# One value product instead of three for the chunk of four left-over keys in a three-layer decoder kernel

## What is computed

```python
xn = _layernorm(x, gamma_media, beta_media)          # context, 6404 rows
ln = _layernorm(latents, gamma_lat, beta_lat)        # the 1024 tokens
q = ln @ Wq + bq
kv_input = jnp.concatenate([xn, ln], axis=1)
kv = kv_input @ Wkv + bkv
k, v = jnp.split(kv, 2, axis=-1)
sim = jnp.einsum('bhid,bhjd->bhij', q * DH ** (-0.5), k)
attn = jax.nn.softmax(sim, axis=-1)
out = jnp.einsum('bhij,bhjd->bhid', attn, v)
```

## Time and profile before

| | us |
|---|---|
| median of 3 runs | 1928.13 |
| lowest and highest run | 1924.66, 1931.77 |
| profiled execution, first to last instruction (span) | 1921.9 |
| TensorE busy in the span | 1815.2 (94%) |
| VectorE busy | 1529.5 (80%) |
| ScalarE busy | 1111.2 (58%) |

### The profile page before, as it was taken

The page is one execution under the profiler, slowest core; times in us unless marked ns, Lnnn a source line. Parts: engine busy times, 40 slices in busy tenths (PEclk is TensorE's granted clock), DMA queues, the critical chain, the costliest instruction groups (busy, mean ns, idle before and its releaser), DMA issues.

```text
span 1921.9 us, 32146 instructions
## 1 busy us (share of the span) xinstructions
PE 1815.2 (94%) x9267; PEld 908.2 (47%) x9267; DVE 1529.5 (80%) x2457; ACT 1111.2 (58%) x1368; POOL 252.0 (13%) x321
## 2 busy tenths in 40 slices
PE   4888889999999999999999999999999999996997
PEld 3775334444444444444444444444444444443554
DVE  6875788888888888888878787879797979546776
ACT  3233256666666666666666666666666666674554
POOL 3911397000000000000000000000000000001554
PEclk7987799999999999999999999999999999997999
DMA  4001020000000000000000000000000000000000
GB/s 124 1 11 33 17 66 21 1 0 0 0 0 0 0 0 0 0 0 0 0 0 0 0 0 0 0 0 0 0 0 0 0 1 0 1 0 1 1 0 11
DMA packets 15350, 13.89 MB, mean 7 GB/s; under 512 B 5839, under 2 KB 13779, under 8 KB 14934
## 3 DMA queue, kind: packets, MB, share of 16 engines
q1 hardware_dynamic: 15318, 13.48, 2.3%
HBM read 12.96 MB, written 0.52 MB: 7 GB/s over the span
## 4 chain that ended last, share of the span: by engine, by line
PE 86%; DVE 8%; issue 3%; ACT 2%; DVEq 0%; DMA 0%; POOLq 0%; POOL 0%; ACTq 0%
PE PS L1105 86%; ACT p_arena L614 1%; DVE mxs L914 1%; DVE w_arena L789 1%; ACT p_arena L607 1%; DVE w_arena L805 0%; DVE mxs L988 0%; DVE w_arena L798 0%; DVE z_arena L1055 0%; DVE w_arena L819 0%; DVE st L867 0%; DVE st L721 0%; DVE w_arena L816 0%; DMA w_arena<-in_x 0%; DVE rs L700 0%
## 5 line engine op out<-in xcount | busy, mean ns | idle before, releaser
L604 ACT ACTIVATE p_arena<-PS 128x1024 f16<-128x1024 f32 (+1 forms) x480 | 484.4, 1009 | 544.3 <-PE PS L1105 544.1
L1105 PE MATMUL PS<-a_arena,z_arena 128*128 (+1 forms) x2832 | 746.4, 380 | 3.8 <-DVE a_arena L933 3.5
L1105 PE MATMUL PS<-p_arena,z_arena 128*128 128x512 f16 x2832 | 747.3, 379 | 1.4 <-ACT p_arena L614 0.3
L940 DVE TENSOR_TENSOR p_arena<-p_arena 128x1024 f16<-128x1024 f32 (+1 forms) x480 | 582.2, 1213 | 134.7 <-ACT p_arena L607 124.6
L914 DVE TENSOR_REDUCE mxs<-PS 128x512 f32 (+1 forms) x900 | 583.2, 667 | 101.1 <-PE PS L1105 98.8
L607 ACT ACTIVATE p_arena<-PS 128x1024 f32<-128x1024 f32 (+1 forms) x480 | 482.0, 1004 | 0.0
L1105 PEld LDWEIGHTS PS<-a_arena,z_arena 128*128 (+1 forms) x2832 | 275.0, 98 | 332.7 <-DVE a_arena L933 4.0
L1105 PEld LDWEIGHTS PS<-p_arena,z_arena 128*128 (+1 forms) x2832 | 272.3, 98 | 316.1 <-ACT p_arena L614 8.8
L1105 PE MATMUL PS<-z_arena,a_arena 128*128 (+3 forms) x1024 | 355.5, 364 | 15.4 <-DVE mxs L914 8.3
L478 POOL TENSOR_TENSOR z_arena<-z_arena 128x512 f16<-128x512 f32 x66 | 76.5, 1159 | 1505.5 <-ACT z_arena L663 1501.5
L1105 PEld LDWEIGHTS PS<-z_arena,a_arena 128*128 (+1 forms) x1024 | 99.0, 98 | 156.4 <-DVE mxs L914 25.1
(11 more groups left out here) (226 smaller groups left out, 965.2 us busy)
## 6 DMA issues: line engine op xcount, KB each, us to landing
w_arena<-in_L_ffn_gate_up_w SPq DMA_DIRECT2D x8, 512.0 KB, 3.7
p_arena<-in_ctx SPq DMA_DIRECT2D x2, 1600.0 KB, 8.4
w_arena<-in_L_ffn_down_w SPq DMA_DIRECT2D x8, 256.0 KB, 4.0
a_arena<-in_L_xattn_Wkv SPq DMA_DIRECT2D x1, 1024.0 KB, 6.7
w_arena<-in_x SPq DMA_DIRECT2D x1, 512.0 KB, 4.3
a_arena<-in_L_xattn_Wo SPq DMA_DIRECT2D x1, 512.0 KB, 7.2
p_arena<-in_L_xattn_Wq SPq DMA_DIRECT2D x1, 512.0 KB
out<-z_arena SPq DMA_DIRECT2D x8, 64.0 KB, 1.6
```

The source lines that it names most:

```text
L604: s.activation(Phi[:, r % 3, 0:w], ps, ACT.Exp, scale=1 / SSC).then_inc(hi_ready, 1)
L940: v.tensor_tensor(Plo[:, r % 3, 0:w], P32[:, r % 2, 0:w], Phi[:, r % 3, 0:w], ALU.subtract).then_inc(lo_ready, 1)
L1105: return t.matmul(o, l, r, start=start, stop=stop)
```

## The change

Chunk 0 holds its four keys three times: in rows 0 to 3, 32 to 35 and 64 to 67. In `Zhi` these rows hold the high part, the low part and the high part again; SyncE copies the two new strips inside the on-chip memory. In `ZThi` and `ZTlo` the four columns are written at columns 0, 32 and 64, so the scores and exponentials of the four keys come out three times too. VectorE then overwrites the third strip of `Phi` (rows 64 to 67) with the low part. One product of `Zhi` chunk 0 with `Phi` gives the three terms at once. It is issued in `values_low`; `values_high` leaves chunk 0 out. `Plo` of chunk 0 is not written any more, so the subtraction of step 0 covers 512 columns instead of 1024. Two semaphores are new: `left_st` (the strips have landed) and `left_lo` (the third strip of `Phi` is written, once per block).

```diff
-        zt_lo_v = sem("zt_lo_v")
+        zt_lo_v, left_st, left_lo = sem("zt_lo_v"), sem("left_st"), sem("left_lo")
...
+        def left_columns(zt):
+
+            return zt[:, 0:96].rearrange("p (g n) -> p g n", n=32)[:, :, 0:LEFT]
...
+            sp.wait_ge(z_lo, 1)
+            sp.dma_start(Zhi[32:32 + LEFT, 0, :], Zlo[0:LEFT, 0, :]).then_inc(left_st, 16)
+            sp.dma_start(Zhi[64:64 + LEFT, 0, :], Zhi[0:LEFT, 0, :]).then_inc(left_st, 16)
             sp.wait_ge(zlT_v, 2)
...
-                    s.copy(dst[:, c0 * P:c0 * P + n], PS[:, 2 + 2 * (i % 2) + o, 0:n]).then_inc(done, 1)
+                    ps = PS[:, 2 + 2 * (i % 2) + o, 0:n]
+                    if c0:
+                        s.copy(dst[:, c0 * P:c0 * P + n], ps).then_inc(done, 1)
+                    else:
+                        s.copy(left_columns(dst), ps.unsqueeze(1).to_broadcast([P, 3, LEFT])).then_inc(done, 1)
...
-                    cols = w * P if c0 else LEFT
-                    v.tensor_copy(ZTlo[:, c0 * P:c0 * P + cols], PS[:, 3 + 2 * (i % 2), 0:cols]).then_inc(zt_lo_v, 1)
+                    ps = PS[:, 3 + 2 * (i % 2), 0:w * P if c0 else LEFT]
+                    if c0:
+                        v.tensor_copy(ZTlo[:, c0 * P:(c0 + w) * P], ps).then_inc(zt_lo_v, 1)
+                    else:
+                        v.tensor_copy(left_columns(ZTlo), ps.unsqueeze(1).to_broadcast([P, 3, LEFT])).then_inc(zt_lo_v, 1)
...
                 dve.wait_ge(p32_ready, g + 1)
-                v.tensor_tensor(Plo[:, r % 3, 0:w], P32[:, r % 2, 0:w], Phi[:, r % 3, 0:w],
+                at = 0
+                if r == 0:
+                    at = QB
+                    rows = slice(64, 64 + LEFT)
+                    v.tensor_tensor(Phi[rows, 0, 0:QB], P32[rows, 0, 0:QB], Phi[rows, 0, 0:QB],
+                                    ALU.subtract).then_inc(left_lo, 1)
+                v.tensor_tensor(Plo[:, r % 3, at:w], P32[:, r % 2, at:w], Phi[:, r % 3, at:w],
                                 ALU.subtract).then_inc(lo_ready, 1)
...
                     o, first, _, zh, zl = sums(r, turn, i)
+                    if STEPS[r][i] == 0:
+                        continue
                     p = Phi[:, r % 3, i * QB:(i + 1) * QB]
...
-            def values_low(g, r, turn=0):
+            def values_low(g, r, turn=0, left=0):
 
                 pe.wait_ge(lo_ready, g + 1)
                 for i in range(len(STEPS[r])):
                     o, _, end, zh, _ = sums(r, turn, i)
+                    if STEPS[r][i] == 0:
+                        pe.wait_ge(left_lo, left + 1)
+                        mm(o, zh, Phi[:, 0, 0:QB], start=True, stop=False)
+                        continue
                     last = mm(o, zh, Plo[:, r % 3, i * QB:(i + 1) * QB], start=False, stop=end)
...
-                        values_low(lagged, lag)
+                        values_low(lagged, lag, left=j)
...
             pe.wait_ge(z_lo, N_HI + 1)
+            pe.wait_ge(left_st, 32)
             pe.wait_ge(a_lo, 2)
```

## The result

| | before | after |
|---|---|---|
| median of 22 runs, us | 1925.66 | 1921.63 |
| lowest and highest run | 1917.17, 1931.99 | 1909.28, 1927.02 |
| profiled span | 1921.9 | 1914.6 |

The ratio is 0.9973 with a 95% interval of 0.9960 to 0.9986. By the ratio that is 5.2 us less, with an interval of 2.7 to 7.7 us; the two medians lie 4.03 us apart. The interval leaves out 1, so the kernel is faster, but by less than the 0.5% that the prediction took as its bound, and by that bound it counts as no change, as forecast. The forecast was 6.1 us less and 1922.0 us.

A forecast was written before the change was run, and what follows sets the result against it. The prediction took TensorE's nearly gapless row of products as the bound, VectorE close behind. 6.9 - 0.3 - 0.5 = 6.1 us gain, from 1928.1 to 1922.0 us; range 1917 to 1930 us.

The forecast's parts named there:

- The price of a product: 512-column value products on TensorE cost 0.216 us each; two fewer save 0.43 us per block, 6.9 us in all.
- The place and the propagation: Products removed in step 2 start step 3 0.43 us sooner; the gain survives the next stop, nothing charged.
- The stop for the sums: TensorE's wait in step 2 for ScalarE's copy of the last block's sums, claimed to stay 0.23 us.
- the stop in the first turn: TensorE's wait for a maximum in the inner loop's first turn, claimed to stay 0.6 us.
- the first rival: Gain given back at the maxima, where VectorE doesn't arrive sooner: 1928.1 us, chance 0.13.
- The subtraction in two: Step 0's subtraction split on VectorE: 0.15 to 0.3 us more per block, hidden in fifteen blocks.
- The cover at the unit: Time between step 1's first maximum on VectorE and the TensorE unit needing it, put at 0.94 us.
- Block 0: First block, without cover at the maximum behind the subtraction: surplus of 0.3 us on the path, once.
- The new wait: Register wait on TensorE's sequencer: 0.03 us per block, 0.5 us in all, bounds 0 and 0.3 us per block.
- The second rival: Sequencer shows: the extra wait stops TensorE for 0.3 us per block, leaving 1.8 us gain, 1926.3 us; chance 0.08.
- Ahead of the blocks: SyncE's two extra transfers, some 0.3 us each, lie within its 80.8 us wait for POOL; costed at nothing.
- The third and fourth rivals: VectorE sets the pace: 1930.5 to 1932.9 us, chance 0.05; remaining product takes the others' time: 1928.1 us, chance 0.02.

The follow-up runs named there:

- v2: Changed kernel with units of the written-out steps 1,2,2,2,2,2,1 instead of 0,2,2,2,2,2,2, wait for A one step earlier: period 94.05 us, time 1924.08 us.
- v3: Changed kernel with units 2,2,2,2,2,2,0, so step 6 has none, and wait for A one step earlier: period 93.98 us, time 1922.17 us.
- v6: v1 with both units of step 6 behind both score groups: period 93.49 us, time 1912.86 us; timed ratio to the kernel before 0.9939.
- v7: v6 with v5's unit numbers, so three units in step 6: period 93.70 us, time 1916.32 us.
- three products again: Changed kernel with chunk 0's product issued three times, the two removed products back: period 94.28 us, time 1928.34 us.
- v1: Changed kernel with the second unit of step 2 ahead of the wait for the copied sums: period 93.71 us, time 1915.36 us.
- v5: v1 with units of the written-out steps 0,2,2,2,2,1,3, one more in step 6: period 93.70 us, time 1920.56 us.

## Why the prediction was right

**The price of a product.** Forecast 0.216 us, 0.43 us a block. The 15 periods give 6.46 / 15 = 0.431 us, and putting the products back gives 94.28 - 93.84 = 0.44 us. The 131 ns for a sustained stream that the Trainium skill gives ("TensorE: Matmul & The Clock Gate", "Back-to-back issue gap") are not borne out here: by them the estimate is 0.26 us a block.

**The place and the propagation.** The stop for the sums stayed 0.24 us and the stop in the first turn 0.60 us, so the first rival (given back at the maxima) is out. The chain of 3.85 us starts at TensorE's own scores. v2, v3 and v6 put numbers to it: with one product less behind those scores (v2) the stop is 0.22 us longer, with one more (v6) 0.21 us shorter. In v3 a unit less stands between the two score groups of step 6 as well, and the stop is v2's, so what counts is the work behind the scores. The prediction made the margin narrower than it was. It saw 0.04 us at 914.69, but VectorE waits for TensorE once more ahead of the stop, in step 5, before the change (first line) and after it (second line):

```profile
920.09 0.69 DVE L914 TENSOR_REDUCE mxs<-PS 128x1 f32<-128x512 f32 x1 [0.88 <-PE PS L1105]
915.88 0.69 DVE L928 TENSOR_REDUCE mxs<-PS 128x1 f32<-128x512 f32 x1 [0.89 <-PE PS L1125]
```

By these rows, a few hundredths lost at the first place would have been caught up at the second.

**The subtraction in two.** Forecast 0.15 to 0.3 us more on VectorE, hidden; measured 0.18 us, hidden in blocks 1 to 15. The overlap of neighbours, 0.07 us, is lost between instructions that begin at different partitions: 0.70 to 0.72 us from start to start, against 0.61 us between two strips at partition 64, and 0.61 us from the 128-row subtraction to the maxima behind it (903.83 to 904.44). With the rule that I cited from the Trainium skill ("VectorE: DVE Perf Modes", "Two Vector instructions with no wait between them") these traces agree. The cover at the unit was sized at 0.94 us ahead of the change, which left 0.94 - 0.18 = 0.76 us; the runs showed 0.67 us, so that term was a tenth of a microsecond too large.

**Block 0.** I charged 0.3 us, because no cover stands there. The changed kernel's profiled run shows none of it. From its timeline of block 0:

```profile
248.42 0.75 DVE L958 TENSOR_TENSOR p_arena<-p_arena 4x512 f16<-4x512 f32 x1 [4.80 <-ACT p_arena L618]
...
249.20 0.77 DVE L960 TENSOR_TENSOR p_arena<-p_arena 128x512 f16<-128x512 f32 x1
249.90 0.75 DVE L928 TENSOR_REDUCE mxs<-PS 128x1 f32<-128x260 f32 x2
250.37 0.29 PE L1125 MATMUL PS<-z_arena,a_arena 128*128 128x256 f16 x2 [1.11 <-DVE mxs L928]
```

The two instructions take 249.90 - 248.42 = 1.48 us, and the stop is 1.11 us where the earlier trace rows have 1.12. Before, the single instruction began at 248.70 and the maxima at 250.18, 1.48 us too. But other traces show the charge. Eight traces are of kernels with the same code up to this stop. In four of them (the changed kernel, v6 twice, v7) it is 1.10 to 1.13 us; in the other four (three products again, the run without the wait, v1, v5) it is 1.38 to 1.40 us, some 0.27 us more than before the change. From the run without the wait:

```profile
249.53 1.04 DVE L958 TENSOR_TENSOR p_arena<-p_arena 4x512 f16<-4x512 f32 x1 [4.80 <-ACT p_arena L618]
250.60 0.77 DVE L960 TENSOR_TENSOR p_arena<-p_arena 128x512 f16<-128x512 f32 x1
```

So the term is nothing in one half of the traces and of its forecast size in the other. What differs is what POOL, at work on the expert weights, is doing: where the strip takes 0.75 to 0.77 us it begins 0.2 us into a short instruction of POOL (line 476), where it takes 1.03 to 1.04 us 0.2 us into a longer one (line 480), and POOL's next instruction takes about twice its usual time in both. In the middle blocks, where POOL does nothing, a strip takes 0.68 us. That POOL is the cause was not tested. Block 0 gained 0.93 us in this trace, but its length was 98.91 us here and 99.80 us without the wait, so half a microsecond there means nothing.

**The new wait.** Charged 0.03 us a block, within 0 to 0.3; measured 0 by the run without it, within the 0.01 us that a period repeats to. The second rival is out.

**Ahead of the blocks.** SyncE's part of the timeline and its wait behind it:

```profile
103.11 0.69 SPq L364 DMA_DIRECT2D z_arena<-z_arena  x1
103.84 0.62 SPq L365 DMA_DIRECT2D z_arena<-z_arena  x1
185.24 0.35 SPq L373 DMA_DIRECT2D w_arena<-in_L_ffn_gate_up_w  x1
...
SPq L367 <- POOL z_arena L464: 80.2, 1, 80.2
```

Each issue took 0.65 us instead of the 0.3 us I wrote, and the wait behind them shrank from 80.8 to 80.2 us: hidden, as forecast.

**The third and fourth rivals** fall with the period of 93.84 us and with the two runs that put products in and take them out. **The numbers:** 6.1 us forecast; taken at their measured values the terms of the sum are 16 x 0.431 = 6.9 us, and losses of nothing or of 0.27 us in block 0. The ratio says 5.2 us with the forecast inside its interval, and the first and second rival (nothing and 1.8 us) outside. That the median came to 1921.63 us, within 0.4 us of the forecast 1922.0, is luck: the forecast started from a median of three runs, 1928.13 us, which is 2.5 us above that of 22, and the medians differ by 2.1 us less than the 6.1 us forecast. One reading of the text was off: I put 6.2 us around the span. The profiled run of the changed kernel took 1916.43 us with a span of 1914.6, so 1.8 us lie around it, and the rest was one run's distance from the median.

## What to carry to other kernels

When one engine issues without gaps, price an instruction by the distance between starts and check each later stop by asking where its chain begins: if it begins at that engine's own work, the stop moves along and the gain survives. Small operands can share a product across partition strips; the extra instruction elsewhere is free only up to the margin of the next consumer, which a run with the cost doubled or tripled measures directly. Stops are shortened by order rather than by amount: produce for the slow chain first and put independent work behind it.

## What the runs showed of the hardware that was not expected

The runs of one kernel differ by up to 18 us, and the blocks have next to no part in it: the 15 periods of v6 sum to 1382.30 us in both of its profiled runs. These two runs, of one kernel on two chips, have spans of 1911.0 and 1918.7 us, and the difference arises ahead of the blocks: the first score product of block 0 started at 243.74 us in the one and at 251.55 us in the other. Busy time by stretch from 100 to 180 us, first the shorter run, then the longer (length, TensorE, its weight loads, VectorE, ScalarE, POOL, granted clock, DMA):

```profile
100.00:180.00 80.00, 70.16 (x356) 52.48 (x355) 52.94 (x177) 23.52 (x75) 11.67 (x12) 0.79 0.02 7
```

```profile
100.00:180.00 80.00, 68.44 (x307) 49.35 (x306) 50.84 (x166) 19.27 (x63) 10.69 (x11) 0.74 0.02 7
```

A mean granted clock of 0.79 against 0.74 goes with 356 against 307 products done by 180 us. Most of the difference arises behind 137 us; the same columns from 137 to 155 us:

```profile
137.00:155.00 18.00, 15.82 (x57) 10.07 (x58) 13.28 (x44) 3.42 (x8) 0.00 (x0) 0.80 0.00 1
```

```profile
137.00:155.00 18.00, 16.10 (x48) 10.30 (x47) 10.10 (x27) 3.42 (x8) 0.00 (x0) 0.54 0.00 0
```

Of the clock's two levels, 2.4 and 1.2 GHz (1.00 and 0.50 in these rows), the shorter run has both here, and the longer stays at the low one nearly throughout. The timed runs of v6, all on one chip, say the same: the four shortest (1906.49 to 1908.41 us) have a mean granted clock of 0.972 to 0.974 over the whole run, the other eight (1912.72 to 1920.55 us) of 0.964 to 0.967. What makes the clock differ from run to run is open. An effect of a few us in the blocks is therefore seen by their period in one run, and by the device time only in many.
